# Scores of a causal attention handed over by PSUM banks, with the causal mask of the second scores as a GpSimd select on the exponentials

## The reference, cut to what matters

```python
x = L0_attn_x                                   # (2, 1024, 128)
xn = _layernorm(x)
x = x + _L0_attn_ref(xn, ...) + _L0_ffn_ref(xn, ...)

def _L0_attn_ref(x, Wq, Wk, Wv, W_O):           # 16 heads of 8 numbers
    Q, K, V = (einsum('bhsd,hde->bhse', xh, W) for W in (Wq, Wk, Wv))
    scores = einsum('bhsd,bhtd->bhst', Q, K) / sqrt(8)
    scores = where(tril(ones((s, s))), scores, -1e9)     # causal
    attn = softmax(scores, axis=-1)
    out = einsum('bhst,bhtd->bhsd', attn, V)
    cat = out.transpose(0, 2, 1, 3).reshape(b, s, e)
    return cat.transpose(0, 2, 1).reshape(b, s, e) @ W_O
```

## Time and profile before

| | |
|---|---|
| Median of 3 runs | 2115.48 us (2111.0 to 2120.15) |
| The profiled execution | 2128.67 us, span 2126.9 us |
| First part | to 382 us of the span |
| Busy share of the span | PE 91%, PEld 62%, DVE 78%, ACT 61%, POOL 67% |
| Longest groups of the first part | L408 gather, L370 and L391 scores, L626 maxima, L868 exponentials |

### The profile page before, as it was taken

How to read it: one execution, slowest core, us unless ns; L and a number is a source line. 1 busy time by engine, 2 the same in 40 slices (tenths; PEclk the granted TensorE clock), 3 DMA queues, 4 the chain that set the end, 5 groups by cost and what they waited for, 6 DMA issues and landing times.

```text
span 2126.9 us, 74573 instructions
## 1 busy us (share of the span) xinstructions
PE 1940.5 (91%) x33032; PEld 1322.8 (62%) x33032; DVE 1658.7 (78%) x1635; ACT 1305.8 (61%) x1547; POOL 1418.3 (67%) x1403
## 2 busy tenths in 40 slices
PE   3989899589999999999899998899999999999985
PEld 1434444357767666776677776667767676676774
DVE  5765562489888888889888988887888888988862
ACT  1355457356667766667666765666776666766752
POOL 1000000699988898879888888597889887888820
PEclk7799999789999999999999999999999999999997
DMA  3141100033233333333223323233333333322221
GB/s 103 39 133 46 44 25 12 28 82 77 70 86 75 87 71 77 90 78 85 63 65 87 91 71 90 49 79 86 74 86 72 79 93 74 72 63 66 69 67 45
DMA packets 144033, 151.51 MB, mean 71 GB/s; under 512 B 60760, under 2 KB 85596, under 8 KB 142944
## 3 DMA queue, kind: packets, MB, share of 16 engines
q1 hardware_dynamic: 143712, 146.75, 27.5%
HBM read 35.75 MB, written 5.44 MB: 19 GB/s over the span
## 4 chain that ended last, share of the span: by engine, by line
PE 32%; DVE 22%; POOL 21%; issue 15%; SPq 5%; ACT 3%; DMA 1%; POOLq 0%; DVEq 0%; ACTq 0%
POOL arena L1109 8%; POOL arena L1117 5%; SPq L1273 4%; DVE arena L626 4%; PE banks L408 4%; DVE ss L713 3%; PE banks L471 3%; PE banks L538 3%; PE banks L480 3%; DVE mx_t L748 3%; PE banks L565 3%; PE banks L391 2%; PE banks L498 2%; DVE arena L721 2%; PE banks L511 2%
## 5 line engine op out<-in xcount | busy, mean ns | idle before, releaser
L1109 POOL TENSOR_TENSOR arena<-arena,tab_sl 128x512 f32<-128x512 f32 x384 | 589.2, 1565 | 16.2 <-ACT arena L917 9.9
L1117 POOL TENSOR_TENSOR arena<-arena 128x1024 f32<-128x1024 f32 x192 | 488.0, 2563 | 0.0
L721 DVE TENSOR_TENSOR arena<-arena,rn 128x1024 f32<-128x1024 f32 x192 | 359.9, 1915 | 113.9 <-POOL rn L1085 113.9
L471 PE MATMUL banks<-w_qkv,arena 128*128 128x512 f32 x768 | 358.4, 609 | 8.3 <-ACT arena L909 5.5
L946 ACT ACTIVATE arena<-arena 128x1024 f32<-128x1024 f32 x96 | 101.6, 1058 | 407.9 <-DVE arena L752 407.9
L626 DVE TENSOR_REDUCE arena<-banks 128x1 f32<-128x1024 f32 (+7 forms) x176 | 175.1, 1027 | 105.1 <-PE banks L372 104.8
L538 PE MATMUL banks<-arena 64*64 64x32 f32 x12288 | 244.0, 222 | 4.0 <-DVE arena L752 3.4
L538 PEld LDWEIGHTS banks<-arena 64*64 64x64 f32 x12288 | 233.2, 135 | 16.9 <-DVE arena L752 5.3
L480 PE MATMUL banks<-ident,arena 128*128 128x128 f32 x1536 | 208.1, 291 | 33.9 <-DVE arena L762 18.5
L471 PEld LDWEIGHTS banks<-w_qkv,arena 128*128 128x128 f32 x768 | 139.4, 191 | 160.0 <-issue 150.8
L762 DVE TENSOR_TENSOR arena<-banks,tab_cl 128x1024 f32<-128x1024 f32 x192 | 226.2, 1219 | 11.8 <-ACT arena L917 10.2
(11 more groups left out here) (108 smaller groups left out, 3067.8 us busy)
## 6 DMA issues: line engine op xcount, KB each, us to landing
arena<-arena SPq DMA_DIRECT2D x1512, 64.0 KB
arena<-parts_dram SPq DMA_DIRECT2D x64, 144.0 KB
w_qkv<-Wqkv SPq DMA_DIRECT2D x6, 1024.0 KB
parts_dram<-arena SPq DMA_DIRECT2D x12, 256.0 KB, 3.1
tab_cl<-tab_c SPq DMA_DIRECT2D x6, 512.0 KB, 7.3
tab_sl<-tab_s SPq DMA_DIRECT2D x6, 512.0 KB
w_o<-Wo SPq DMA_DIRECT2D x6, 512.0 KB
w_qkv<-Wqkv SPq DMA_DIRECT2D x6, 512.0 KB, 4.6
```

What stands on the lines that cost most here:

```text
L471: last = e.matmul(ps[:, BANK * c:BANK * (c + 1)], xsT[b][:, P * t:P * (t + 1)], w_qkv[:, at:at + BANK], start=True, stop=True)
L721: e.tensor_tensor(to, to, rn[n // 2 % 2][:, n % 2, HEADS * m:HEADS * (m + 1)].unsqueeze(2).to_broadcast([P, HEADS, HEAD_DIM]), ALU.mult).t ...
L1109: e.tensor_tensor(qk_sw[:, m, :].rearrange("p (h d) -> p h d", d=HEAD_DIM)[:, :, d:d + HALF], raw[:, m, :].rearrange("p (h d) -> p h d", d ...
L1117: e.tensor_tensor(to, to, qk_sw[:, m, :], ALU.add).then_inc(S["rs"], 1)
```

## The change

1. **By banks.** `pieces` cuts a unit into its two banks: for a unit of one head, columns 0 to 511 and the rest; for two or four heads, half of the heads each. TensorE raises `a_sc` and `a_wsc` after each bank, VectorE and ScalarE read each bank with an instruction of its own, and a later use waits for the two banks of a pair one at a time (`place(..., by_bank=True)`, `pair(..., bank=)`). For one head of query tiles 4 to 7 the maximum now comes out as two halves, `m_first` and `m_neg`; `a_maxima_split` joins them with one more operation.
2. **The second mask.** The matmuls of L393 go. GpSimd sets the masked part of the exponentials to zero, in place, once for each key tile (four heads x 128 columns), after its last exponential. The gather takes the second 512 query columns first where there are two chunks, and waits for the select (`a_causal`) only ahead of the chunk with the diagonal.
3. GpSimd scales the tables (L1043, L1051) after its 64 selects instead of before.

```diff
 
+        def pieces(j, many, n, bank):
+
+            if many == 1:
+                return slice(j, j + 1), BANK * bank, min(n, BANK * (bank + 1))
+            return slice(j + bank * many // 2, j + (bank + 1) * many // 2), 0, n
...
-        def place(use, n_pairs, *readers):
+        def place(use, n_pairs, *readers, by_bank=False):
             i = turns.n % n_pairs
             turns.up()
             pair_of[use], before[use] = i, last_on.get(i)
-            last_on[i] = [readers[k:k + 2] for k in range(0, len(readers), 2)]
+            whole = [readers[k:k + 2] for k in range(0, len(readers), 2)]
+            first = [(done, count - 1) for done, count in whole] if by_bank else whole
+            last_on[i] = (first, whole)
...
-                place(("a_sc", k), 3, "a_max", k + 1)
+                place(("a_sc", k), 3, "a_max", 2 * k + 2, by_bank=True)
...
-            def pair(*use):
-                for done, count in before[use] or []:
-                    w.wait_ge(S[done], count)
+            def pair(*use, bank=1):
+                if before[use]:
+                    for done, count in before[use][bank]:
+                        w.wait_ge(S[done], count)
                 return banks[:, pair_of[use], :]
...
-                ps = pair("a_sc", k)
                 w.wait_ge(S["masks_b"], 1)
-                for i in range(many):
-                    slot, at = slot_of(g, j0 + i), apart * i
-                    w.wait_ge(stack_in[slot], STACK_DMAS * 16 * (g // 3 + 1))
-                    for c in range((n + BANK - 1) // BANK):
-                        end = min(n, BANK * (c + 1))
-                        e.matmul(ps[:, at + BANK * c:at + end], QS[slot][0:ROWS, P * qt:P * (qt + 1)],
-                                 KS[slot][0:ROWS, BANK * c:end], start=True, stop=True)
-                    last = e.matmul(ps[:, at + n - P:at + n], ident_b, mask_rows, start=False, stop=True, skip_group_check=True)
-                last.then_inc(S["a_sc"], 1)
+                for bank in range(2):
+                    heads, c0, c1 = pieces(j0, many, n, bank)
+                    ps = pair("a_sc", k, bank=bank)
+                    for j in range(heads.start, heads.stop):
+                        slot, at = slot_of(g, j), apart * (j - j0)
+                        w.wait_ge(stack_in[slot], STACK_DMAS * 16 * (g // 3 + 1))
+                        last = e.matmul(ps[:, at + c0:at + c1], QS[slot][0:ROWS, P * qt:P * (qt + 1)],
+                                        KS[slot][0:ROWS, c0:c1], start=True, stop=True)
+                        if c1 == n:
+                            last = e.matmul(ps[:, at + n - P:at + n], ident_b, mask_rows, start=False, stop=True, skip_group_check=True)
+                    last.then_inc(S["a_sc"], 1)
...
-                ps = pair("a_wsc", s)
                 w.wait_ge(S["ones_out"], 16 * RING)
-                for i in range(many):
-                    slot, at = slot_of(g, j0 + i), apart * i
-                    w.wait_ge(rows_in[slot], 16 * (g // 3 + 1))
-                    for c in range((n + BANK - 1) // BANK):
-                        end = min(n, BANK * (c + 1))
-                        e.matmul(ps[:, at + BANK * c:at + end], KS[slot][0:ROWS + PARTS, q0:q0 + P],
-                                 QS[slot][0:ROWS + PARTS, q0 + BANK * c:q0 + end], start=True, stop=True)
-                    last = e.matmul(ps[:, at:at + P], ident_b, mask_cols, start=False, stop=True, skip_group_check=True)
-                last.then_inc(S["a_wsc"], 1)
+                for bank in range(2):
+                    heads, c0, c1 = pieces(j0, many, n, bank)
+                    ps = pair("a_wsc", s, bank=bank)
+                    for j in range(heads.start, heads.stop):
+                        slot, at = slot_of(g, j), apart * (j - j0)
+                        w.wait_ge(rows_in[slot], 16 * (g // 3 + 1))
+                        last = e.matmul(ps[:, at + c0:at + c1], KS[slot][0:ROWS + PARTS, q0:q0 + P],
+                                        QS[slot][0:ROWS + PARTS, q0 + c0:q0 + c1], start=True, stop=True)
+                    last.then_inc(S["a_wsc"], 1)
...
-                w.wait_ge(S["a_exp"], g * UNITS + last_unit[kt] + 1)
+                w.wait_ge(S["a_exp"], 2 * (g * UNITS + last_unit[kt] + 1))
                 if kt == 0 and g:
                     w.wait_ge(S["a_acc"], g)
-                for c in range(seq // BANK):
+                for c in reversed(range(seq // BANK)):
                     if q0 < BANK * (c + 1):
                         s0 = max(q0, BANK * c)
+                        if s0 == q0:
+                            w.wait_ge(S["a_causal"], quad + 1)
                         for j in range(A_PER_GROUP):
                             h = g % A_GROUPS * A_PER_GROUP + j
                             last = e.matmul(banks[A_SLOT * j:A_SLOT * (j + 1), 3, s0:BANK * (c + 1)], VA[:, kt, h, :],
...
-                w.wait_ge(S["a_sc"], k + 1)
                 if g >= 2:
                     w.wait_ge(S["a_mlo"], g - 1)
-                e.tensor_reduce(m_neg[g % 2][:, qt, j0:j0 + many],
-                                banks[:, pair_of["a_sc", k], :].rearrange("p (j n) -> p j n", j=many)[:, :, 0:n],
-                                AX_X, ALU.max, negate=True).then_inc(S["a_max"], 1)
+                for bank in range(2):
+                    heads, c0, c1 = pieces(j0, many, n, bank)
+                    to = m_first[g % 2][:, qt - tiles // 2, heads] if c1 < n else m_neg[g % 2][:, qt, heads]
+                    w.wait_ge(S["a_sc"], 2 * k + bank + 1)
+                    e.tensor_reduce(to, banks[:, pair_of["a_sc", k], BANK * bank:BANK * (bank + 1)].rearrange(
+                        "p (j n) -> p j n", j=heads.stop - heads.start)[:, :, 0:c1 - c0], AX_X, ALU.max, negate=True).then_inc(S["a_max"], 1)
...
-                w.wait_ge(S["a_max"], (g + 1) * UNITS)
+                w.wait_ge(S["a_max"], 2 * (g + 1) * UNITS)
+                upper = m_neg[g % 2][:, tiles // 2:tiles, :]
+                e.tensor_tensor(upper, upper, m_first[g % 2], ALU.min).then_inc(S["a_mstep"], 1)
+                w.wait_ge(S["a_mstep"], 4 * g + 1)
                 w.wait_ge(S["a_mT"], max(0, g - 1))
                 e.tensor_copy(mp[:, :, 0, :], m).then_inc(S["a_mstep"], 1)
-                w.wait_ge(S["a_mstep"], 3 * g + 1)
+                w.wait_ge(S["a_mstep"], 4 * g + 2)
...
-                w.wait_ge(S["a_wsc"], s + 1)
                 w.wait_ge(S["a_gather"], max(0, quad - 1))
-                e.activation(pt_ring[quad % 2][:, j0:j0 + many, 0:n],
-                             banks[:, pair_of["a_wsc", s], :].rearrange("p (j n) -> p j n", j=many)[:, :, 0:n], ACT.Exp,
-                             scale=float(A_DIM) ** -0.5).then_inc(S["a_exp"], 1)
+                for bank in range(2):
+                    heads, c0, c1 = pieces(j0, many, n, bank)
+                    w.wait_ge(S["a_wsc"], 2 * s + bank + 1)
+                    e.activation(pt_ring[quad % 2][:, heads, c0:c1],
+                                 banks[:, pair_of["a_wsc", s], BANK * bank:BANK * (bank + 1)].rearrange(
+                                     "p (j n) -> p j n", j=heads.stop - heads.start)[:, :, 0:c1 - c0], ACT.Exp,
+                                 scale=float(A_DIM) ** -0.5).then_inc(S["a_exp"], 1)
...
+            zero = e.to_reg(0.0)
+            for quad in range(a_groups * tiles):
+                g, kt = divmod(quad, tiles)
+                w.wait_ge(S["a_exp"], 2 * (g * UNITS + last_unit[kt] + 1))
+                own = pt_ring[quad % 2][:, :, 0:P]
+                e.affine_select(own, own, [[0, A_PER_GROUP], [1, P]], ALU.is_ge, zero, base=0, channel_multiplier=-1
+                                ).then_inc(S["a_causal"], 1)
+                w.wait_ge(S["a_causal"], quad + 1)
             scale_cos(0)
             scale_sin(0)
```

More of the change, by code:

```diff
@@ L99 @@
 ln_step ln_var ln_root x_norm masks_b wdiag ones_set a_xT a_xnT a_proj a_hi a_rest a_mid a_lo a_vproj a_va va_set
-a_sc a_max a_mstep a_mlo a_mT a_mrows a_wsc a_exp a_gather a_acc a_accT a_recip a_cat a_out a_y
+a_sc a_max a_mstep a_mlo a_mT a_mrows a_wsc a_exp a_causal a_gather a_acc a_accT a_recip a_cat a_out a_y
 tab_c tab_s halves_set zero_xs zero_xf row_in xsT xs_ready proj raw sq ss_sum newton rn rc sw rs rot tk tq kt_ready qt_ready kp
@@ L124, in build @@
         banks = ctx.enter_context(nc.psum_tensor("banks", [P, 4, PAIR], F32))
-        ARENA = 37 * PAIR + 128
+        ARENA = 37 * PAIR + 160
         arena = sb("arena", [P, ARENA])
@@ L187, in build @@
         m_neg = [carve("A", tiles * A_PER_GROUP).rearrange("p (t j) -> p t j", j=A_PER_GROUP) for _ in range(2)]
+        m_first = [carve("A", tiles // 2 * A_PER_GROUP).rearrange("p (t j) -> p t j", j=A_PER_GROUP) for _ in range(2)]
         M_ROWS = A_PER_GROUP * PARTS * tiles
@@ L283, in build @@
             if 0 <= s < units:
-                place(("a_wsc", s), 3, "a_exp", s + 1)
```

(16 more changed lines are left out.)

## The result

The changed kernel takes 2081.8 us (median of 4 runs, 2080.19 to 2091.56) against 2113.24 us of the kernel before: ratio 0.9859, 95% interval 0.9816 to 0.9901. Forecast were 2092.5 us and a range of 2076 to 2119. A later comparison on another chip gave 2096.1 us of 12 runs, ratio 0.9922 (0.9892 to 0.9952). By medians that is a gain of 14.6 us, where the first comparison had 31.4. The two intervals just overlap, and the better estimate, from both together, is a gain of about 1%, some 21 us.

A forecast was written before the change was run, and what follows sets the result against it. TensorE and the hand-over of whole pairs bound the kernel. 6.5 groups x -4.5 = -29 us, +2 first scores alone, -0.6 half-clock stretch, +4.3 end: -23, so 2115.5 - 23 = 2092.5 us, range 2076 to 2119.

The forecast's parts named there:

- the end of the first part: Last groups, without first scores: the select's wait shows there, less the saved masks; net +4.3 us.
- rival C: TensorE's clock: with fewer gaps its drops may go, -32 us in all, 2083 us; chance 0.14.
- Bound by TensorE and the hand-over of pairs: Full-clock group with both scores: some 30.2 us of TensorE work in 36.2, 6 us of gaps from whole-pair hand-over.
- Masks, 1.7 us per group: Second scores: 32 mask matmuls of 53 ns each, all on TensorE's own path, save 1.7 us per group.
- The walk: TensorE timed from key tile 2's gather to the group's transpose: 2.7 us saved there, 4.5 us per whole group.
- VectorE's price of splitting: VectorE's reductions: a unit cut in two costs 0.07 us more back to back, 0.16 where it waits in between.
- the stage of first scores alone: Opening stage, bound by VectorE: thirty split units at 0.07 us, minus an earlier first reduction, make it 2 us longer.
- The select, 1.2 us: GpSimd's masking of each key tile: taken at 1.2 us, between bounds of 0.44 and 2.5 us.
- the estimate of -17 us: The sum if the first gather waits once for a GpSimd instruction-memory load of about 6 us.
- Rival A: Ends of groups: selects of 2.5 us hold TensorE up, sum about +25 us, 2141 us; chance 0.14.
- if the second part has moved by more than 5 us, my sum is of the wrong place: Sign for the unchanged second part: it should stay at 1744 us, within 5 us.

The follow-up runs named there:

- Banks only: The changed kernel without its select: second mask again a matmul inside its bank, gather in the old order; 33.02 us per full-clock group, ratio 0.9902, again 0.9878.
- Four selects: The changed kernel with the select done four times in a row on each key tile; ratio 1.0227 to the kernel before.

## Why the prediction was right, step by step

The direction, the place and the mechanism held. The size, 23 us, lies between the two timed gains of 31.4 and 14.6 and near the 21 of both together. That it does is in part luck: two terms were mis-sized in opposite directions (the masks in the groups gave less, the end of the first part cost less), and the first median, 2081.8, stands next to the 2083 of rival C.

- **Bound by TensorE and the hand-over of pairs:** shown. Banks only gives 3.17 us per group; my 4.5 less the masks' share of 1.4 to 1.7 had 2.8 to 3.1 for it.
- **Masks, 1.7 us per group, "in place of work and not of a gap":** this step failed. They give 0.87 us, and beside it the second scores' wait for VectorE grew from 1.0 to 2.1 us. Together with the clock and the end of the first part, the select's half of the change brought nothing measurable in time. Had I asked what TensorE would wait for next, VectorE's release was the row to look at.
- **The walk:** 4.5 us per group forecast, 4.04 measured. The stretch that it walked, from the gather of kt 2, ended after 18.09 us (275.17 to 293.26), not 17.6: the gathers of kt 3 to 7 began at 4.7, 7.8, 10.7, 12.4 and 13.9 us, 0.1 us late at first and 0.7 us late from kt 6 on. The rest of the group gave 1.8 us (15.86 to 14.06), as forecast.
- **VectorE's price of splitting, 0.07 us per unit back to back:** 38 reductions in 18.54 us for the 19 units that took 17.36, 0.06 each (first row below). In the groups the price was taken too high: VectorE's busy time rose from 23.45 to 24.63 us, 0.05 per unit, and ScalarE's from 19.97 to 20.62, where I had some 27 and 23.5. And the stage of first scores alone did not get 2 us longer: its reductions began earlier (45.09, before 47.39; 46.30 in the second profile), and the first matmul of the second scores came at 72.3 us, before 73.4 (73.6 in the second profile).

```profile
45.09 18.54 DVE L642 TENSOR_REDUCE arena<-banks 128x1 f32<-128x512 f32 x38 [1.28 <-PE banks L381]
```

- **The select, 1.2 us:** mis-sized, 0.64. With it the end of the first part cost less than the 4.3 us I charged: the stretch after the sixth transpose, forecast 2.3 us longer (4.3, less 2.0 for the 16 us of it that have both scores), came out 0.5 shorter. The first select has no extra wait: it starts at 79.50 us, 0.15 us after ScalarE's exponentials (78.27 + 1.08), and takes 0.64 us. So the load of about 6 us in the Trainium skill (GPSIMD Engine Reference, Instruction dispatch), and the estimate of -17 us with it, did not apply here. The same page's Engine selection calls one-input operations on GpSimd roughly line-rate; the trace agrees, with 0.64 us for 512 columns beside 0.69 for a reduction of as many on VectorE.
- **Rival A** was priced for a select of 2.5 us. Four selects put it to the test: 43 us slower than the kernel before on the same chip (2149.65 against 2106.49), 2.3%, where +25 was named (its own terms, +34 and +17 on -23, add up to +28). The mechanism is real, but A put no price on the clock, and that the 2149.65 stands close to its 2141 says little. The chip's own select stays far from it.
- **Rival C** (fewer clock drops) is half true. In the profile after, 6.4 of the 26.6 us in the five groups are the clock's, where the sum had 0. Against the trace of the kernel before, that is most of the 8 us that the forecast lacked; but against both timed comparisons together it lacked nothing.
- **A bad test of mine:** "if the second part has moved by more than 5 us, my sum is of the wrong place". It moved by 6.2 us and meant nothing, since the same code took 1738 and 1728 us in two profiles of one kernel.
- **The chances:** A had 0.14 with half of it at less than +10 us, which leaves 0.07 for times above 2126, and not the 0.13 that were given.

## What to carry to other kernels

Where an engine waits for a buffer of several banks and its reader is quick, let reader and writer hand over bank by bank; with slack on the reader, its added cost (0.06 us per unit here) is small beside the wait (up to 0.6 us each in the kernel before). Work taken off the bounding engine may count only in part (here about half); look for the next release that it waits for before counting the removed instructions in full. When the rest of a program scatters by more than the effect, compare stretches of the traces between two fixed events, and trace each kernel more than once, the kernel before too: here it has one trace, and some 8 us of the traced difference don't appear in the timed one.

## What was not expected of the hardware

The granted clock could take back, or add, as much as the smaller half of the change. Equal groups of the kernel before took 36.19 us at 1.00 and 40.59 at 0.87, and of the changed kernel 32.15 at 1.00 and 33.62 at 0.95. In the one place read closely, a stretch in which TensorE had waited stood before the drop: 2.96 us busy of 4 in the earlier trace rows. The share of time at 1.2 GHz differs between executions of one kernel. The 12 later ones of the changed kernel took 2078 to 2105 us; the two fastest had a mean granted clock of 0.961 and 0.962, the three slowest 0.955 to 0.958. What decides when a drop comes stays open here.
